# Stores in one row, loads on a second queue, zeros sent early and the choice of experts moved in an attention and mixture-of-experts kernel

## The chip, the core and the metric

The kernel runs on one core of a Trainium2 chip. The metric is the time of one execution in microseconds (us) on the device, taken in three runs; one further execution was recorded by the hardware profiler. The core has five engines with their own instruction streams: TensorE (PE, matmuls), VectorE (DVE), ScalarE (ACT), GpSimd (POOL) and SyncE (SP, which here only issues transfers). They meet through semaphores. Transfers are issued from SP, ACT or POOL and run on 16 DMA engines. PSUM has eight banks of 128 x 512 numbers.

## What is computed

The input `x` has 2 x 1024 tokens of width 256. From its layer norm `xn` two things are computed and both are added to `x`.

```python
qkv = xn @ qkv_w.T + qkv_b                       # 16 heads of 16
scores = einsum(q, k) / 4 + slope * (key - query), causal
x += softmax(scores) @ v @ out_w.T + out_b
# mixture of experts on the same xn
scores = sigmoid(xn @ gate_w)                    # 16 experts
selected = top_k(scores + expert_bias, 2)
w = scores[selected] / scores[selected].sum()
x += silu(xn @ shared_gate) * (xn @ shared_up) @ shared_down
x += sum over the two selected: w * (silu(xn @ g_e) * (xn @ u_e)) @ down_e
```

## The kernel before

The program is written out by hand for each engine; the order of each stream is the order of the code, and only semaphores tie the streams.

**Projections.** A list `JOBS` gives PE's work in turn, with one PSUM bank for each job: transposed weights and tokens, then 16 jobs of kind `qk` (one of q or k, 128 features, 512 tokens each), eight of `v`, four of the router's logits `g` and one of their transposes `r`. Each q/k result is split into three bf16 parts, so that bf16 matmuls keep f32 accuracy. ACT makes the first two parts (L594, L602), DVE the rest and the third (L750, L713). They stand in `parts`, a ring of `RING = 6` slots; SP stores slot `i % 6` to DRAM (`store_parts`, L379), and ACT may write part `i` only when store `i - 6` has landed.

**Head groups.** The 16 heads of two sequences are handled in `NG = 8` groups of four heads. For a group `load_group` brings the parts back in a layout in which one contraction over 108 or 111 rows holds all products of parts, the alibi terms and the negated row maximum (L337 and L339, 192, 128 and 64 KB and the alibi rows for each of q and k). It loads the first 512 positions and then the second, each with a semaphore of its own. Three buffers take the groups in turn. A group's maxima come first: PE computes scores (L1124, L1125), DVE reduces them (L888), DVE negates and splits the result (`negate`, L896 to L903), and SP writes it into three rows of the q buffer (`store_neg`, L408). Then PE computes the scores anew with the maximum subtracted (`exp_scores`, L1136), ACT takes the exponential (L665), and PE multiplies by the values (`weigh`, L1150). `ORDER` mixes, on PE and DVE, the exponential scores of group g with the maxima of group g + 1 and the first three (`EARLY`) of g + 2. Maxima have two slots in PSUM, so PE runs at most two ahead of DVE.

**Experts.** `route` on DVE picks two experts for each token and computes the two gates; `rank` on PE counts tokens by expert; `place` on DVE turns this into a row for each token and choice (`slot_i`) and an expert for each of the 48 tiles (`eid`). `sorted_tokens` is filled with zeros by 12 transfers (L402), POOL then scatters the tokens into it with 32 indirect transfers (L525), and after head groups 0 and 1 PE runs the 48 tiles. The shared expert (`shared_gate_up`, `shared_down`) is computed between the router and the attention, mixed with the maxima of group 0. The router's small tiles share SBUF with `ot_soon`, into which ACT evacuates attention outputs (`evacuate`, L669).

**SP's order** before the experts: constants, alibi rows, stores 0 to 5, load of group 0, stores 6 to 9, load of group 1, stores 10 to 15, zeros, negated rows of group 0, load of group 2, `w_gu` (the experts' first weights, 4 MB), negated rows of group 1, a wait for the scatters, `w_dn` (2 MB), four token tiles, load of group 3, negated rows of group 2.

## Time and profile before

| | us |
|---|---|
| three runs | 559.04, 561.94, 566.04 |
| median | 561.94 |
| profiled execution | 566.61 |
| its span, first to last instruction | 564.8 |
| PE busy | 476.7 (84%) |
| DVE busy | 327.7 (58%) |
| ACT busy | 247.5 (44%) |
| POOL busy | 141.3 (25%) |
| mean granted clock of TensorE | 0.906 |

The span is divided by the work into stages: projections to about 92 us, router to 110, shared expert and maxima of group 0 to 151, head groups 0 and 1 to 232, experts to 326, head groups 2 to 7 to about 533, and the output projection. A busy share is an average over these stages; which engine or queue sets the end of one is seen in the chain that ended last and in the waits of that stage. A releaser (`<-`) names what ended an engine's idle time. Lines such as L594 are lines of the kernel before.

### The profile page before, as it was taken

How to read it: one execution, taken by the hardware profiler on the slowest of the kernel's cores; microseconds unless marked ns; L12 is line 12 of the kernel's file. 1: busy time of each engine (PE TensorE's matmuls, PEld its weight loads, DVE VectorE, ACT ScalarE, POOL GpSimd, SP SyncE). 2: the span in 40 equal slices, each digit the busy share in tenths (PEclk: the TensorE clock that was granted, in tenths of full speed). 3: DMA queues.
4: the chain of work that ended last, by engine and by line, in shares of the span. 5: the costliest groups of instructions: out<-in, count | busy, mean ns of one | idle time of the engine just before them, and what ended most of it. 6: DMA issues, size and time to landing. Idle time of an engine off the chain costs nothing.

```text
span 564.8 us, 8563 instructions
## 1 busy us (share of the span) xinstructions
PE 476.7 (84%) x3049; PEld 271.4 (48%) x3049; DVE 327.7 (58%) x605; ACT 247.5 (44%) x567; POOL 141.3 (25%) x167
## 2 busy tenths in 40 slices
PE   4698069287599299799999999799999999699998
PEld 3587066154243143577777643344444353221476
DVE  4874076968867267354544477477776768422232
ACT  2663040000067167443444366466766767534400
POOL 2550000027740000000000058188875700000000
PEclk9799578689789789999999999799999999955899
DMA  9554433953334942144444233232332200010022
GB/s 274 92 167 127 130 107 123 387 198 110 107 130 124 310 156 75 54 150 141 139 141 140 94 103 109 76 110 58 111 99 84 88 12 1 4 13 0 2 76 75
DMA packets 64260, 63.53 MB, mean 112 GB/s; under 512 B 15295, under 2 KB 59907, under 8 KB 64219
## 3 DMA queue, kind: packets, MB, share of 16 engines
q1 hardware_dynamic: 60042, 54.18, 31.5%
q0 software_dynamic: 3072, 8.39, 4.6%
q8 instruction: 26, 0.43, 0.3%
q10 hardware_dynamic: 1104, 0.41, 0.3%
q14 instruction: 16, 0.12, 0.1%
HBM read 36.29 MB, written 26.15 MB: 111 GB/s over the span
## 4 chain that ended last, share of the span: by engine, by line
PE 65%; DVE 16%; DMA 7%; SPq 7%; ACT 3%; issue 2%; DVEq 0%; ACTq 0%
PE ps L1136 11%; PE ps L1150 11%; PE ps L1124 11%; PE ps L1074 9%; DVE mx L888 6%; PE ps L1170 5%; PE ps L1090 4%; SPq L337 4%; DMA qk<-nr 4%; SPq L408 2%; PE ps L974 2%; PE ps L1125 2%; PE ps L1139 2%; DMA qk_parts<-parts 2%; PE ps L1064 2%
## 5 line engine op out<-in xcount | busy, mean ns | idle before, releaser
L665 ACT ACTIVATE pt<-ps 128x512 f32<-128x512 f32 (+3 forms) x384 | 167.1, 492 | 132.3 <-PE ps L1139 103.8
L888 DVE TENSOR_REDUCE mx<-ps 128x1 f32<-128x384 f32 (+7 forms) x216 | 178.6, 864 | 71.4 <-PE ps L1125 69.4
L1136 PE MATMUL ps<-qk 111*128 111x512 bf16 (+3 forms) x384 | 117.0, 350 | 19.4 <-DMA qk<-nr 17.9
L1124 PE MATMUL ps<-qk 108*128 108x512 bf16 (+3 forms) x384 | 105.2, 342 | 9.5 <-DVE mx L888 8.9
L1150 PE MATMUL ps<-pt,vg 128*32 128x512 f32 (+3 forms) x768 | 86.8, 529 | 0.0
L1136 PEld LDWEIGHTS ps<-qk 111*128 111x128 bf16 x384 | 37.0, 101 | 72.5 <-ACT pt L665 23.8
L1124 PEld LDWEIGHTS ps<-qk 108*128 108x128 bf16 x384 | 32.7, 101 | 66.3 <-DVE mx L888 46.9
L541 POOL DMA_INDIRECT yg<-sorted_outputs,slot_i x32 | 32.3, 1011 | 104.7 <-DMA sorted_outputs<-y_out 96.5
L1125 PE MATMUL ps<-cbf 128*128 128x128 bf16 x256 | 56.0, 231 | 0.0
L1074 PE MATMUL ps<-w_gu,hx 128*128 x192 | 53.3, 401 | 2.0 <-ACT hx L633 1.3
L1139 PE MATMUL ps<-cbf 128*128 128x128 bf16 x256 | 54.2, 229 | 0.0
L876 DVE COPY y_out<-ps 128x256 f32<-128x256 f32 x48 | 20.4, 425 | 44.8 <-PE ps L1090 44.8
L525 POOL DMA_INDIRECT sorted_tokens<-xn,slot_i x32 | 31.0, 969 | 45.6 <-DMA sorted_tokens<-zeros 36.1
L514 POOL COPY vg<-v_sb 128x512 f32<-128x512 f32 x8 | 4.8, 609 | 143.0 <-PE ps L1150 94.2
L1074 PEld LDWEIGHTS ps<-w_gu,hx 128*128 128x128 f32 x192 | 32.5, 189 | 11.8 <-issue 8.0
L649 ACT ACTIVATE hx<-ps 128x384 f32<-128x384 f32 (+1 forms) x48 | 22.9, 477 | 26.1 <-PE ps L1064 24.5
L1125 PEld LDWEIGHTS ps<-cbf 128*128 128x128 bf16 x256 | 26.4, 103 | 15.9 <-issue 0.5
L1090 PE MATMUL ps<-w_dn,hx 128*128 x96 | 31.2, 406 | 0.9 <-ACT hx L649 0.9
L556 POOL TENSOR_SCALAR yg<-yg,gates 128x256 f32<-128x256 f32 x32 | 30.0, 938 | 3.4 <-DMA yg<-sorted_outputs,slot_i 2.2
L750 DVE SCALAR_TENSOR_TENSOR part_r<-ps,qkb,parts 128x512 f32<-128x512 f32 x16 | 11.9, 750 | 28.4 <-ACT parts L594 24.1
L974 PE MATMUL ps<-wh,xl 128*128 128x256 f32 x32 | 10.0, 313 | 21.1 <-DVE part_r L750 21.1
L1150 PEld LDWEIGHTS ps<-pt,vg 128*32 128x32 f32 x768 | 15.5, 111 | 22.7 <-ACT pt L665 16.1
(160 smaller groups left out, 577.4 us busy)
## 6 DMA issues: line engine op xcount, KB each, us to landing
qk_parts<-parts SPq DMA_DIRECT2D x16, 384.0 KB, 6.7
qk<-qk_parts SPq DMA_DIRECT2D x32, 192.0 KB
sorted_tokens<-zeros SPq DMA_DIRECT2D x12, 512.0 KB, 6.0
x_in<-sorted_tokens SPq DMA_DIRECT2D x48, 128.0 KB, 2.2
sorted_outputs<-y_out SPq DMA_DIRECT2D x48, 128.0 KB, 1.7
qk<-qk_parts SPq DMA_DIRECT2D x32, 128.0 KB
w_gu<-e_gu SPq DMA_DIRECT2D x1, 4096.0 KB, 19.4
x_sb<-x SPq DMA_DIRECT2D x4, 512.0 KB, 8.7
```

The source lines that it names most:

```text
L525: g_.indirect_dma_start(out=xsd, out_offset=bass.IndirectOffsetOnAxis(ap=slot_i[:, k, t:t + 1], axis=0), in_=xn[:, t, :], in_offset=None). ...
L541: g_.indirect_dma_start(out=yg[:, n % 4, :], out_offset=None, in_=ysd, in_offset=bass.IndirectOffsetOnAxis(ap=slot_i[:, k, t:t + 1], axis= ...
L556: g_.tensor_scalar(yg[:, n % 4, :], yg[:, n % 4, :], gates[:, k, t:t + 1], None, ALU.mult).then_inc(s_gw, 1)
L665: sc.activation(pt[:, s % 2, j, lo:CH], bank(n % 3)[:, lo:CH], ACT.Exp).then_inc(s_exp, 1)
L888: last = v.reduce_max(dst, src, axis=AX.X)
L1074: ins = te.matmul(bank(2 + w, 2 * F), hx[:, 1 - w, 1 + c, :], w_gu[:, bass.ds(e, 1), c, :].rearrange("p o f -> p (o f)"), start=c == 0, st ...
L1090: te.matmul(bank(4 + w, D), hx[:, w, 0, :], w_dn[:, bass.ds(e, 1), :].rearrange("p o f -> p (o f)"), start=True, stop=True).then_inc(s_dn, 1)
L1124: te.matmul(ps[:, at + c:at + e], q, k_buf[g % NBUF][0:K_MAX, j, c:e], start=True, stop=e < w)
L1125: ins = te.matmul(ps[:, at + w - P:at + w], idb, mask_q, start=False, stop=True)
L1136: ins = te.matmul(out[:, lo:CH], k_buf[g % NBUF][0:K_EXP, j, kb * P:(kb + 1) * P], q_buf[g % NBUF][0:K_EXP, j, qc * CH + lo:(qc + 1) * CH] ...
L1139: ins = te.matmul(out[:, lo:lo + P], idb, mask_k, start=False, stop=True)
L1150: ins = te.matmul(ps[32 * j:32 * j + 32, OUT_BANK * CH + lo:(OUT_BANK + 1) * CH], vg[:, par, kb, j, :], pt[:, s % 2, j, lo:CH], start=kb = ...
```

## The change

1. SP issues all 16 stores of q/k parts in one row. The loads of groups 0 and 1 are issued by POOL, once stores 0 to 3 and the alibi rows have landed, with semaphores of their own.
2. A load moves whole rows of 1024 positions: eight transfers for a group instead of 16, and PE waits once for all eight.
3. The zeros are issued before the alibi rows and the parts, once the constants have landed.
4. `route` and `place` on DVE come after the negation of group 0, `rank` on PE after the first eight exponential score blocks of group 0, in the PSUM bank of the attention output. `FIRST_ORDER` puts the maxima of group 1 that stood before that point behind it. DVE copies the ranks out of PSUM first.
5. The gates' sums over experts are made by POOL in ten small steps (`gate_sums`), and the division by their sum by four steps of DVE at the start of `experts`.

```diff
+RANKS_AT = ORDER.index(("out", 1))
+FIRST_ORDER = ([x for x in ORDER[:RANKS_AT] if x[0] != "max"] + [("rank", 0)] + [("max", 1, p) for p in range(EARLY)]
+               + [x for x in ORDER[:RANKS_AT] if x[0] == "max"] + ORDER[RANKS_AT:])
...
-        s_ld = [[sem(f"half{half}_loaded{n}") for n in range(NBUF)] for half in range(2)]
+        s_first = [sem(f"first_rows_loaded{n}") for n in range(NBUF - 1)]
+        s_ld = [sem(f"rows_loaded{n}") for n in range(NBUF)]
...
-        def load(queue, side, g, half):
+        def load(queue, side, g):
...
                 if side == 0:
-                    src = qkd[0, p0:p0 + 1, g:g + 1, :, :, cols].rearrange("n g d j s -> (g n) d j s")
-                    src = src.broadcast_to([n, HD, HG, CH])
+                    src = qkd[0, p0:p0 + 1, g:g + 1].rearrange("n g d j s -> (g n) d j s")
+                    src = src.broadcast_to([n, HD, HG, S])
...
+        def await_rows(queue, g):
+            if g < NBUF - 1:
+                queue.wait_ge(s_first[g], LOADS * DMA)
+            else:
+                queue.wait_ge(s_ld[g % NBUF], (g // NBUF + (g % NBUF == NBUF - 1)) * (LOADS * DMA))
...
             sp.dma_start(wsd[:, :], sd_w).then_inc(s_wo, DMA)
 
+            sp.wait_ge(s_zero, 2)
+            sp.wait_ge(s_c, DMA * N_CONST)
+            sp.wait_ge(s_wo, 4 * DMA)
+            sp.wait_ge(s_ws, 3 * DMA)
+            xz = xsd.rearrange("(p k) d -> p (k d)", p=P)
+            for n in range(NT // 4):
+                sp.dma_start(xz[:, n * 4 * D:(n + 1) * 4 * D], zeros[:, :, :].rearrange("p k d -> p (k d)")
+                             ).then_inc(s_clear, DMA)
...
-                for half in range(2):
-                    for side in range(2):
-                        load(sp, side, g, half)
+                for side in range(2):
+                    load(sp, side, g)
 
-            for i in range(RING):
+            for i in range(NQK):
                 store_parts(i)
             sp.wait_ge(s_auxst, 4 * DMA)
-            for i in range(4):
-                sp.wait_ge(s_parts[i], DMA)
-            load_group(0)
-            for i in range(RING, RING + 4):
-                store_parts(i)
-            load_group(1)
-            for i in range(RING + 4, NQK):
-                store_parts(i)
...
+            def gate_sums():
+                pool.wait_ge(s_picked, 1)
+                for k in range(K_TOP):
+                    summing(g_.tensor_tensor(weight[:, :, :], pick[:, k, :, :], prob[:, :, :], ALU.mult))
+                    for w in (E // 2, E // 4, E // 8):
+                        summing(g_.tensor_tensor(weight[:, :, 0:w], weight[:, :, 0:w], weight[:, :, w:2 * w], ALU.add))
+                    summing(g_.tensor_tensor(gates[:, k, :].unsqueeze(2), weight[:, :, 0:1], weight[:, :, 1:2], ALU.add))
...
+            pool.wait_ge(s_auxst, 4 * DMA)
+            for i in range(4):
+                pool.wait_ge(s_parts[i], DMA)
+            for g in range(NBUF - 1):
+                for side in range(2):
+                    load(pool, side, g)
             pool.wait_ge(s_free, JOBS.index(("g", 0, 0)))
             copy_v(0)
             copy_v(1)
 
+            gate_sums()
             pool.wait_ge(s_slot, 1)
...
             def evacuate(g, qc):
+                if g == 0 and qc == 0:
+                    act.wait_ge(s_slot, 2)
+                    act.wait_ge(s_gsum, GATE_STEPS)
...
                 dve.wait_ge(s_rank, 1)
-                ranks = bank(R0 % 8)
+                v.tensor_copy(ranks[:, :], bank(OUT_BANK, TT * E + E)).then_inc(s_ranks, 1)
+                dve.wait_ge(s_ranks, 1)
...
             def experts():
+                dve.wait_ge(s_gsum, GATE_STEPS)
+                v.scalar_tensor_tensor(gsum[:, 0, :], gates[:, 0, :], 1e-20, gates[:, 1, :], ALU.add, ALU.add
+                                       ).then_inc(s_gate, 1)
...
+            route()
+            place()
             for p in range(EARLY):
                 maxima(1, 1, p)
...
-                    for kind, a, b in [(*x, 0)[:3] for x in ORDER]:
+                    for kind, a, b in [(*x, 0)[:3] for x in (ORDER if g + par else FIRST_ORDER)]:
+                        if kind == "rank":
+                            rank()
+                            await_rows(pe, 1)
...
-                            if b in (0, FIRST_HALF):
-                                pe.wait_ge(s_ld[int(b > 0)][n % NBUF], (n // NBUF + 1) * (LOADS * DMA))
+                            if b == 0 and n > 1:
+                                await_rows(pe, n)
...
             shared_gate_up(0)
             shared_gate_up(1)
-            rank()
...
-                    pe.wait_ge(s_free, NJ)
-                    for half in range(2):
-                        pe.wait_ge(s_ld[half][0], LOADS * DMA)
+                    pe.wait_ge(s_free, NJ - 1)
+                    pe.wait_ge(s_prob, 1)
+                    await_rows(pe, 0)
```

**Order on SP**, the projections. `parts` are the stores, `qk<-qk_parts` the loads, `zeros` the clearing of the sorted tokens. Before:

```order
L371 DMA aux_rows<-aux 120x1024 [waits aux_ready] x4
L379 DMA qk_parts<-parts 128x3x512 [waits parts_ready] x6
L337 DMA qk<-qk_parts 48x4x512 [waits parts_stored2,parts_stored1,parts_stored3,parts_stored0,aux_stored]
...
L379 DMA qk_parts<-parts 128x3x512 [waits parts_ready] x4
L337 DMA qk<-qk_parts 48x4x512
...
L379 DMA qk_parts<-parts 128x3x512 [waits parts_ready] x6
L402 DMA sorted_tokens<-zeros 128x1024 [waits zeroed]
L402 DMA sorted_tokens<-zeros 128x1024 x11
L408 DMA qk<-nr 1x32x128 [waits neg_ready]
```

With the change, up to the wait of `w_dn`:

```order
L384 DMA wsd<-sd_w 128x256
L392 DMA sorted_tokens<-zeros 128x1024 [waits wo_loaded,small_weights_loaded,consts_loaded,zeroed]
L392 DMA sorted_tokens<-zeros 128x1024 x11
L397 DMA aux_rows<-aux 120x1024 [waits aux_ready] x4
L405 DMA qk_parts<-parts 128x3x512 [waits parts_ready] x16
L419 DMA qk<-nr 1x32x128 [waits neg_ready,aux_stored]
...
L445 DMA w_gu<-e_gu 128x32x256
L419 DMA qk<-nr 1x32x128 [waits neg_ready]
L419 DMA qk<-nr 1x32x128 x2
L448 DMA w_dn<-e_dn 128x16x256 [waits tokens_sorted]
```

The loads of groups 0 and 1 are gone from SP, the zeros stand ahead of the alibi rows and the 16 stores are in one row; `w_dn` waits for the scatters as it did before.

**Order on DVE**, from the logits to the first maxima of group 1. `rt<-prob` begins the choice, `slot_i` ends the placing of tokens. Before:

```order
L758 TENSOR_TENSOR v_sb<-ps,vb 128x2x4x64 [waits job_ready] x8
L741 COPY logits_t<-ps 16x512 [waits job_ready] x4
L784 TENSOR_SCALAR rt<-prob 128x256 [waits router_exp_ready,job_ready]
L785 RECIPROCAL prob<-rt 128x256 [waits router_step]
L786 TENSOR_TENSOR biased<-prob,eb 128x256 [waits router_step]
...
L822 CAST slot_i<-slot_f 128x32 [waits router_step]
L824 TENSOR_TENSOR etab<-cnt,row 128x768
L825 TENSOR_REDUCE eid_f<-etab 128x48 [waits router_step]
L826 TENSOR_SCALAR eid<-eid_f 128x48 [waits router_step]
L853 SCALAR_TENSOR_TENSOR th<-th,ps 128x512 [waits shared_tanh_ready]
L858 SCALAR_TENSOR_TENSOR hsh<-th,ps 128x512 [waits shared_step]
```

With the change (L885 and L890 are the shared hidden steps, L943 ends the negation of group 0, L928 are maxima):

```order
L796 TENSOR_TENSOR v_sb<-ps,vb 128x2x4x64 [waits job_ready] x8
L782 COPY logits_t<-ps 16x512 [waits job_ready] x4
L885 SCALAR_TENSOR_TENSOR th<-th,ps 128x512 [waits shared_tanh_ready]
L890 SCALAR_TENSOR_TENSOR hsh<-th,ps 128x512 [waits shared_step]
...
L943 TENSOR_TENSOR nr<-nrf,nr 32x128 [waits neg_step]
L822 TENSOR_SCALAR rt<-prob 128x256 [waits router_exp_ready]
L823 RECIPROCAL prob<-rt 128x256 [waits router_step]
...
L854 CAST slot_i<-slot_f 128x32 [waits router_step]
L856 TENSOR_TENSOR etab<-cnt,row 128x768
L857 TENSOR_REDUCE eid_f<-etab 128x48 [waits router_step]
L858 TENSOR_SCALAR eid<-eid_f 128x48 [waits router_step]
L928 TENSOR_REDUCE mx<-ps 128x4 [waits max_scores_ready]
```

The choice and the placing have moved from ahead of the shared expert to behind the negation of group 0.

**Order on PE**, the start of head group 0. L1136 and L1178 are exponential scores, L1124 and L1166 maxima of group 1, L1150 and L1194 `weigh`, L1025 the ranks. Before:

```order
L1136 MATMUL ps<-qk 128x512 [waits exp_done,vg_ready,neg_loaded0]
L1139 MATMUL ps<-cbf 128x128
L1124 MATMUL ps<-qk 128x384 [waits max_slot_freed]
L1125 MATMUL ps<-cbf 128x128
L1124 MATMUL ps<-qk 128x384 [waits max_slot_freed]
L1125 MATMUL ps<-cbf 128x128
L1136 MATMUL ps<-qk 128x512 [waits exp_done]
L1139 MATMUL ps<-cbf 128x128
...
L1136 MATMUL ps<-qk 128x384 [waits exp_done]
L1139 MATMUL ps<-cbf 128x128
L1150 MATMUL ps<-pt,vg 32x512 [waits out_evacuated,exp_done]
L1150 MATMUL ps<-pt,vg 32x512 x3
```

With the change:

```order
L1178 MATMUL ps<-qk 128x384 [waits exp_done]
L1181 MATMUL ps<-cbf 128x128
L1178 MATMUL ps<-qk 128x384 [waits exp_done]
...
L1025 MATMUL ps<-picked,cbf 128x16 [waits picked_ready,consts_loaded]
L1025 MATMUL ps<-picked,cbf 128x16 x15
L1027 MATMUL ps<-picked,cbf 128x256
...
L1166 MATMUL ps<-qk 128x128 [waits max_slot_freed,first_rows_loaded1]
L1167 MATMUL ps<-cbf 128x128
...
L1166 MATMUL ps<-qk 128x512 [waits max_slot_freed]
L1167 MATMUL ps<-cbf 128x128
L1194 MATMUL ps<-pt,vg 32x512 [waits ranks_evacuated,out_evacuated,exp_done]
L1194 MATMUL ps<-pt,vg 32x512 x3
```

Ten maxima of group 1, of which three stood ahead of the first exponential scores and seven between the eight blocks, now stand together between the ranks and the first `weigh`.

## Rows read from the trace of the kernel before

**Rows 1.** ACT timeline: start us, length us, engine, line, what, [idle before <- releaser]
```profile
40.45 0.69 ACT L594 ACTIVATE parts<-ps,qkb 128x512 bf16<-128x512 f32 x1 [3.42 <-DMA qk_parts<-parts]
...
46.99 0.67 ACT L594 ACTIVATE parts<-ps,qkb 128x512 bf16<-128x512 f32 x1
...
73.27 0.69 ACT L594 ACTIVATE parts<-ps,qkb 128x512 bf16<-128x512 f32 x1 [24.69 <-DMA qk_parts<-parts]
...
76.84 0.67 ACT L594 ACTIVATE parts<-ps,qkb 128x512 bf16<-128x512 f32 x1
...
99.35 0.60 ACT L628 ACTIVATE th<-ps 128x512 f32<-128x512 f32 x1 [2.19 <-PE ps L974]
```

**Rows 2.** SP queue timeline (issues of transfers), same columns, first 116 us
```profile
19.89 0.46 SPq L366 DMA_DIRECT2D wsd<-sd_w  x1
...
43.64 2.79 SPq L337 DMA_DIRECT2D qk<-qk_parts  x3
...
100.74 14.59 SPq L402 DMA_DIRECT2D sorted_tokens<-zeros  x12
```

**Rows 3.** Windows: stretch and length us, PE busy, PE clock, DMA share, GB/s
```profile
40.00:45.00 5.00, 5.00 (x24) 1.00 1.00 344
...
49.80:66.00 16.20, 3.97 (x34) 0.76 0.23 70
...
100.00:118.00 18.00, 7.59 (x58) 0.62 1.03 396
```

**Rows 4.** DMA issues: out<-in, queue, count, KB each, median us to landing
```profile
wsd<-sd_w SPq DMA_DIRECT2D x1, 128.0 KB, 3.4
...
qk<-nr SPq DMA_DIRECT2D x24, 8.0 KB, 1.9
...
sorted_tokens<-xn,slot_i POOLq DMA_INDIRECT x32, 2.4
```

**Rows 5.** DVE timeline, from the router to the first negated maxima
```profile
92.51 0.29 DVE L784 TENSOR_SCALAR rt<-prob 128x256 f32<-128x256 f32 x1 [1.82 <-ACT prob L586]
...
100.11 0.42 DVE L796 TENSOR_TENSOR picked<-pick 128x256 bf16<-128x256 f32 x1
...
107.72 0.18 DVE L822 CAST slot_i<-slot_f 128x32 int32<-128x32 f32 x1
...
109.89 0.68 DVE L853 SCALAR_TENSOR_TENSOR th<-th,ps 128x512 f32<-128x512 f32 x1
...
116.02 4.08 DVE L888 TENSOR_REDUCE mx<-ps 128x4 f32<-128x512 f32 x7 [0.16 <-PE ps L1125]
...
151.15 0.28 DVE L903 TENSOR_TENSOR nr<-nrf,nr 32x128 bf16<-32x128 f32 x1
```

**Rows 6.** PE timeline in the first two head groups
```profile
154.77 0.61 PE L1136 MATMUL ps<-qk 111*128 111x512 bf16 x1 [1.85 <-DMA qk<-nr]
...
161.39 1.06 PE L1150 MATMUL ps<-pt,vg 128*32 128x512 f32 x8
...
226.95 0.22 PE L1124 MATMUL ps<-qk 108*128 108x128 bf16 x1
```

**Rows 7.** SP queue timeline in the first two head groups
```profile
185.40 7.33 SPq L408 DMA_DIRECT2D qk<-nr  x3
...
192.77 0.58 SPq L437 DMA_DIRECT2D w_dn<-e_dn  x1
...
224.34 0.58 SPq L339 DMA_DIRECT2D qk<-aux_rows  x1
```

**Rows 8.** POOL timeline: first and last of the 32 scatters
```profile
122.77 1.23 POOL L525 DMA_INDIRECT sorted_tokens<-xn,slot_i  x1 [36.12 <-DMA sorted_tokens<-zeros]
...
162.26 0.96 POOL L525 DMA_INDIRECT sorted_tokens<-xn,slot_i  x1 [0.30 <-issue]
```

**Rows 9.** Chain that ended last: start us, length us, what
```profile
192.14 6.09 DMA qk<-nr
...
355.08 4.43 DMA qk<-nr
```

More of the change, by code:

```diff
@@ L1148, in weigh @@
                     pe.wait_ge(s_ev, g * 2 + qc + 1)
+                if g == 0 and s == 0:
+                    pe.wait_ge(s_ranks, 1)
                 for j in range(HG):
@@ L1204, in _ @@
                 if c == 0:
-                    pe.wait_ge(s_free, NJ)
-                    for half in range(2):
-                        pe.wait_ge(s_ld[half][0], LOADS * DMA)
+                    pe.wait_ge(s_free, NJ - 1)
+                    pe.wait_ge(s_prob, 1)
+                    await_rows(pe, 0)
                 for p in range(c * NP // 4, (c + 1) * NP // 4):
                     max_scores(0, 0, p)
-            for half in range(2):
-                pe.wait_ge(s_ld[half][1], LOADS * DMA)
-            for p in range(EARLY):
-                max_scores(1, 1, p)
             for g in range(0, NG, 2):
```

59 lines of the change are left out of this document (31 added, 28 removed).

## The prediction

> **What bounds the kernel now.** I read the page's chain that ended last first: PE carries most of it, so I looked in time order for its pieces that are not arithmetic. There are four. The longest is in the projections. ACT has all six slots of `parts` full and waits 24.69 us for a q/k part to be stored [rows 1]. SP, which issues the stores, is busy at that time with the 16 loads of head group 0 that it issues between store 5 and store 6; the first three are in [rows 2]. These loads move little: between 49.8 and 66 us the DMA engines are 23% busy at 70 GB/s, while six stores on their own run them full at 344 GB/s and the zeros at 396 [rows 3]. The reader should see a queue whose order costs time, not a lack of bandwidth. The second piece is the router on DVE, from 92.51 to 109.89 us [rows 5]; PE and ACT have nothing else for most of it. The third and fourth are waits of PE for the three small rows of negated maxima, which are queued behind large transfers: 6.09 and 4.43 us of transfer where 1.9 is the median [rows 4, 9].
>
> All times below are of the profiled execution, 566.6 us (span 564.8). It lies 0.8% above the median of the three runs, 561.94; the result is scaled to that at the end. N is the end of the first negation, 151.4 us before [rows 5].
>
> **1. Zeros ahead of the parts: a cost of 5 us.** The last constant before them is issued at 19.89 and lands 3.4 us after the issue ends [rows 2, 4], so the zeros start at about 23.8. They are 12 x 524 KB = 6.3 MB; at 396 GB/s [rows 3] that is 15.9 us, to 39.7. Behind them in the same queue go 0.98 MB of alibi rows (2.9 us at 344) and store 0 (1.1 us), then the landing, 1.9 us by the small stores of [rows 4]. Part 6 can start at about 46 instead of 40.45 [rows 1]. The scatter's old wait for the zeros, 36.12 us on POOL [rows 8], goes, but that POOL wait bounded nothing.
>
> **2. Stores in a row: a gain.** From part 6 on DVE sets the pace: from part 6 to part 11 it is 6.5 us (40.45 to 46.99 [rows 1]), and for the next four steps I take 1.5 each, a little over the mean of 1.3, so part 15 would start at 46 + 6.5 + 6 = 58.5 against 76.84: 18.3 us earlier. This is the lower bound of the cost. But POOL starts the 16 loads of groups 0 and 1 when parts 0 to 3 have landed, at about 49.5, and 3.5 MB then shares the engines with ten stores of 0.39 MB. All of that at 344 GB/s is 21.5 us, so if the stores came last, part 15 would start at 71, a gain of 5.8. The stores go out at 0.39 MB per 1.5 us, 260 GB/s, and need three quarters of the engines' time; I take 5 us of delay, nearer to the free end, since the loads of before left 77% of the engines idle. **Gain 13.3**, between 5.8 and 18.3. The loads themselves are hidden: POOL has 0.96 us per scatter and 1.27 from one to the next [rows 8]; 16 direct transfers at one to three times that are issued by 70 to 110, and group 0 is first read at about 90, group 1 at about 136.
>
> **3. The router leaves the front: a gain.** After the router's exponentials DVE now takes the shared hidden part at once. The second tanh ends at 99.95 [rows 1], the step that it feeds was reached at 111.2 (109.89 and two steps of the first tanh), and two additions and the first maxima follow at 116.02 [rows 5]. With PE no longer idle ahead of the shared down matmuls, that 116.02 becomes about 102.8. **Gain 13.2** (11 to 15). So N moves from 151.4 to 151.4 - 26.5 = 124.9.
>
> **4. The router in head group 0: a cost.** DVE needs 8.0 us up to `picked` and 9.4 from there to the end of the placing (109.89 - 100.53 [rows 5]); the gate products go to POOL, but the rank matmuls and a copy out of PSUM, once beside them, fill that time. PE meanwhile has only eight score blocks, after the 3.3 us of the negated rows' store (151.43 to 154.77 [rows 6]). Then it meets ten maxima in a row with two PSUM slots: the tenth needs eight reductions, 4.7 us by the seven in 4.08 of [rows 5], and its matmul. `weigh` of step 0 comes at N + 8.0 + 9.4 + 4.7 + 0.5 = N + 22.6, where it was N + 10.0 (161.39 [rows 6]). With 1 us for PE at the lower clock after its idle time: **cost 13.6** (11 to 17). Moving the router is thus nearly a wash.
>
> **5. The second group's negated rows: a gain.** Before, the negated rows of group 1 were issued from 185.40 on [rows 7], behind the 4.2 MB of `w_gu`, and landed at 198.2 (192.14 + 6.09 [rows 9]): 12.9 us after their negation instead of 3.3. Now that negation ends at N + 34.0 + 13.6 = N + 47.6. The load of group 2 starts at N + 2 and takes some 25 us (1.75 MB at 70 GB/s [rows 3]), `w_gu` behind it 12.2 at 344 GB/s and 2 to land, so it is through by about N + 41. **Gain 9.6** (5 to 9.6).
>
> **6. The load of group 3: a cost that the diff does not show.** The scatters now start after `slot_i`, at N + 8.0 + 7.2 = N + 15.2, and 32 of them take 40.5 us (122.77 to 163.2 [rows 8]), plus 2.4 to land [rows 4]: N + 58. SP waits for this before `w_dn`, and the load of group 3 stands behind. Before, the way from `w_dn` to the end of that load's issue was 192.77 to 224.92 [rows 7], 32.2 us, of which up to 4.8 were the rest of `w_gu`; with 27.4 to 32.2 and 1.9 of landing the rows are there at N + 87 to N + 92. PE asks for them at its first maxima of group 3, 75.5 us after N before (226.95 [rows 6]), now N + 75.5 + 13.6 - 9.6 = N + 79.5. Before, the first half sufficed there; now one semaphore counts all eight transfers. **Cost 9** (3 to 13).
>
> The load's size in time is the question. A row that bears on it is the 23% of [rows 3]: under four of 16 engines busy. The Trainium skill, "DMA: Bandwidth & Descriptors", section on why a DMA increments its semaphore by 16, says that a transfer runs on the largest number of engines up to 16 that divides the slowest dimension of both sides, here the leading 3 and 2 copies. The trace agrees (0.23 x 16 = 3.7). By that rule whole rows change nothing in the spread, and the load keeps its 25 us (1.75 MB at the 70 GB/s of [rows 3]).
>
> **7. Later groups.** The load of group 4 ended just ahead of the negated rows of group 3 and cost them 2.5 us (4.43 against 1.9 [rows 4, 9]); with half as many transfers I take it to be through. **Gain 2.5** (0 to 2.5; below zero by 2 if the whole load is late at the early maxima). Four small gate steps on DVE before the experts are hidden under the first token transposes and gate matmuls of PE, and ACT's new wait for POOL's ten small steps ends by N + 20: nothing. Were that cover gone they would cost some 1 us.
>
> **Sum:** -13.3 - 13.2 + 13.6 - 9.6 + 9 - 2.5 = -16.0, so 550.6; times 561.94 / 566.6 it is 546, and I forecast **547**.
>
> **Rivals.**
> - *The load is quick.* If the 23% came from 1 KB rows and not from the shape, a load with 8 KB rows takes 1.75 MB / 344 GB/s = 5 us, group 3 is in time and term 6 is gone: 566.6 - 25 = 541.6, **537** scaled. For it: the zeros' 4 KB rows moved at 396 against 344. Against it: that is 15%, not fivefold.
> - *Little is left.* Stores and loads share badly (5.8 instead of 13.3) and the load of group 3 is at its late end (12.5): -16 + 7.5 + 3.5 = -5, **557**. For it: both terms lean on estimates, and each stands at one place of the chain.
> - *POOL's loads starve the stores*: slower. A store needs all its engines; if an engine gives most of its turns to the 8 KB rows of a load, ten stores wait until the loads are through. At 25 us for a group two groups end at 49.5 + 50 = 99.5, part 15 starts at about 98, 21 us later than before instead of 13.3 earlier: 566.6 - 16 + 34.5 = 585, **580** scaled. It turns the sign once part 15 starts after 79.5, and passes 2% after 91. Against it: POOL's queue would have to put all these loads on the same few engines. The same page, section on queues, rings and completion order, says that an engine goes round its queues by packets; no row before shows two queues at full load.
> - *The change does not do what it says*: if part 6 to 15 still wait for something else on SP, gain 2 vanishes; SP's order leaves nothing there.
>
> **How the numbers follow.** My forecast has 0.52, with 540 to 555 of its own from the bounds of its terms; the quick load 0.14; little left 0.24; starved stores 0.08; the rest 0.02. The range 535 to 560 leaves out the starved case and the tails. About 2% (11.2 us, below 550.7) is what a measurement can tell from no change. Faster by that: 0.42 of the forecast, all of the quick load, 0.02 of little left, 0.58. Slower: 0.08. Within: 0.34.
>
> **What would show it.** Right: ACT's idle time before part 15 falls from 24.69 to under 15 us in all, and part 15 starts near 63; the first maxima near 90; a PE gap of some 7 us inside group 0 ended by DVE; no long wait for the negated rows of group 1; a PE wait of about 9 us for a transfer of `qk` ahead of the experts. Wrong: an ACT wait on stores while POOL's loads run that lasts beyond 79 us; maxima of group 0 or 1 that wait for rows; no wait ahead of the experts (quick load), or one over 13 us.

## The result, and the profile after

The changed kernel takes 588.88 us (median of four runs, 582.76 to 595.06) where the kernel before takes 561.32 (four runs, 559.04 to 566.04): ratio 1.0443, 95% interval 1.0325 to 1.0562. It is slower; I had forecast 547. Here and below, executions over 1.5% above the fastest of the same kernel stand in the medians and not in the ratios. The profiled execution took 582.76 us (span 580.8 against 564.8: 16.0 us more).

Part of what I expected is there: the first negation comes 17.9 us earlier, where I had 26.5. The loss is later. It is seen at once in the chain that ended last (page, part 4; before, PE had 65% and transfers 7%):

```profile
PE 40%; DMA 30%; DVE 9%; POOL 8%; SPq 7%; issue 4%; ACT 1%; DVEq 0%; ACTq 0%; POOLq 0%
DMA qk<-aux_rows 24%; PE ps L1116 9%; POOL sorted_tokens L560 5%; PE ps L1214 5%; PE ps L1194 5%; PE ps L1132 4%; PE ps L1178 4%; DMA qk_parts<-parts 4%; DVE mx L928 4%; PE ps L1016 3%; SPq L348 3%; PE ps L1166 3%; POOL aux L538 2%; PE ps L1106 2%; DMA eb<-ebias 1%
```

`qk<-aux_rows` is the last of a group's eight transfers, so it stands for the whole load. In the chain it has five pieces, one each for groups 3 to 7 (start, length, what):

```profile
200.95 26.77 DMA qk<-aux_rows
332.89 27.84 DMA qk<-aux_rows
370.07 27.84 DMA qk<-aux_rows
407.39 28.51 DMA qk<-aux_rows
445.23 26.34 DMA qk<-aux_rows
```

These lengths run from the issue of the last transfer. SP's queue, here for group 4, shows the first issue 4.3 us earlier, and the next load 37.2 us later:

```profile
328.59 1.94 SPq L348 DMA_DIRECT2D qk<-qk_parts  x3
...
332.89 0.53 SPq L350 DMA_DIRECT2D qk<-aux_rows  x1
...
365.79 1.93 SPq L348 DMA_DIRECT2D qk<-qk_parts  x3
```

PE's timeline has the waits at the first maxima of groups 3 to 7, 25.7 us in all:

```profile
227.76 0.29 PE L1166 MATMUL ps<-qk 108*128 108x128 bf16 x1 [8.73 <-DMA qk<-aux_rows]
...
360.78 0.29 PE L1166 MATMUL ps<-qk 108*128 108x128 bf16 x1 [5.36 <-DMA qk<-aux_rows]
...
397.97 0.29 PE L1166 MATMUL ps<-qk 108*128 108x128 bf16 x1 [4.12 <-DMA qk<-aux_rows]
```

The reader should see a closed loop. A load lasts 4.3 + 27.8 = 32.1 us. PE starts the next group's maxima only when all of it is there (360.7), needs 5.1 us from there until SP may overwrite the oldest buffer (365.79), and the next load begins. 32.1 + 5.1 = 37.2 us a group, and a faster PE could shorten only the 5.1. Before, from group 4 on, a group took 31.5: the negations of groups 5 to 7 ended at 422.1, 453.8 and 485.2 (that of group 4 at 390.7). DVE's timeline before has

```profile
421.79 0.28 DVE L903 TENSOR_TENSOR nr<-nrf,nr 32x128 bf16<-32x128 f32 x1
453.54 0.28 DVE L903 TENSOR_TENSOR nr<-nrf,nr 32x128 bf16<-32x128 f32 x1
484.88 0.28 DVE L903 TENSOR_TENSOR nr<-nrf,nr 32x128 bf16<-32x128 f32 x1
```

and now, for groups 3 to 7,

```profile
356.57 0.30 DVE L943 TENSOR_TENSOR nr<-nrf,nr 32x128 bf16<-32x128 f32 x1
...
394.58 0.33 DVE L943 TENSOR_TENSOR nr<-nrf,nr 32x128 bf16<-32x128 f32 x1
432.01 0.28 DVE L943 TENSOR_TENSOR nr<-nrf,nr 32x128 bf16<-32x128 f32 x1
469.74 0.28 DVE L943 TENSOR_TENSOR nr<-nrf,nr 32x128 bf16<-32x128 f32 x1
506.00 0.28 DVE L943 TENSOR_TENSOR nr<-nrf,nr 32x128 bf16<-32x128 f32 x1
```

The difference of the two spans by stage, from negation to negation (the first ends at N, 151.4 before and 133.5 after; differences of the unrounded times):

| stage | before | after | difference |
|---|---|---|---|
| start to N | 151.4 | 133.5 | -17.9 |
| to the negation of group 1 | 33.9 | 49.2 | +15.2 |
| to group 2 | 42.8 | 37.3 | -5.4 |
| to group 3 (experts between) | 125.7 | 136.8 | +11.1 |
| to group 7 | 131.3 | 149.4 | +18.1 |
| to the end | 79.7 | 74.6 | -5.1 |
| sum | 564.8 | 580.8 | +16.0 |

Of the 18.1 up to group 7 only 1.2 are in the first round, from group 3 to group 4: it took 36.9 us already before, where PE waited for negated rows (4.43 us of transfer [rows 9]), and 38.0 after. The other three rounds cost 16.9.

The gain at the end is TensorE's clock. PE is busy throughout 30 us of it in both kernels (501 to 531 before, 522 to 552 after); before, the granted clock was 0.50 in the first 15 of them (the level of 1.2 GHz) and 0.67 in the rest, after it was 0.55 and then 1.00 (2.4 GHz). Nothing of the change stands there, and a second trace of the changed kernel, `e15_change_again`, has 76.1 us for this stage.

In the projections the store waits of ACT, which answer to [rows 1], are

```profile
45.62 0.69 ACT L630 ACTIVATE parts<-ps,qkb 128x512 bf16<-128x512 f32 x1 [8.12 <-DMA qk_parts<-parts]
...
63.16 0.69 ACT L630 ACTIVATE parts<-ps,qkb 128x512 bf16<-128x512 f32 x1 [7.93 <-DMA qk_parts<-parts]
71.27 0.69 ACT L630 ACTIVATE parts<-ps,qkb 128x512 bf16<-128x512 f32 x1 [6.91 <-DMA qk_parts<-parts]
73.16 0.69 ACT L630 ACTIVATE parts<-ps,qkb 128x512 bf16<-128x512 f32 x1 [0.69 <-DMA qk_parts<-parts]
```

The wait before part 6 has grown from 3.42 us to 8.12, which is the price of the early zeros. The one wait of 24.69 us behind it is replaced by three that sum to 15.5, and part 15 starts at 73.16, 3.7 us earlier than before. What the DMA engines do meanwhile, by queue, from 49 to 70 us (packets, MB, share of the 16 engines), and the issues in that stretch:

```profile
q0 software_dynamic: 1971, 2.96, 50.3%
q1 hardware_dynamic: 2625, 2.58, 39.9%
...
qk_parts<-parts SPq DMA_DIRECT2D x7, 384.0 KB, 18.8
qk<-qk_parts POOLq DMA_DIRECT2D x4, 384.0 KB, 6.7
```

From POOL's queue the loads take half of all engines: the four transfers of 384 KB land in 6.7 us (median; the smaller ones in 8.3 to 19.3), while a store needs 18.8. On SP transfers with the same leading dimensions had left 77% of the engines idle [rows 3]. The packets of 4 and 8 KB in the trace hint at how. On POOL's queue five are under way at once for most of the first 1.6 us (its first two transfers have leading 3 and 2), and up to 15 in the next microseconds; of SP's load of group 5 there are two or three for most of the time from 374 to 397 us, never over five. That fits transfers that still use few engines each, but stand side by side on different ones; no run tests it alone.

### The profile page after: what moved, and what is told of

The parts are those of the page before. It is cut to its first block, busy times and chain, and to the rows that moved or that the text cites. A ratio compares the mean times of both kernels' runs of the same rounds, so it can differ in the third digit from the quotient of the medians.

```text
span 580.8 us, 8502 instructions
## 1 busy us (share of the span) xinstructions
PE 482.8 (83%) x3049; PEld 274.5 (47%) x3049; DVE 327.6 (56%) x602; ACT 246.9 (43%) x567; POOL 155.1 (27%) x193
## 4 chain that ended last, share of the span: by engine, by line
PE 40%; DMA 30%; DVE 9%; POOL 8%; SPq 7%; issue 4%; ACT 1%; DVEq 0%; ACTq 0%; POOLq 0%
DMA qk<-aux_rows 24%; PE ps L1116 9%; POOL sorted_tokens L560 5%; PE ps L1214 5%; PE ps L1194 5%; PE ps L1132 4%; PE ps L1178 4%; DMA qk_parts<-parts 4%; DVE mx L928 4%; PE ps L1016 3%; SPq L348 3%; PE ps L1166 3%; POOL aux L538 2%; PE ps L1106 2%; DMA eb<-ebias 1%
## 5 line engine op out<-in xcount | busy, mean ns | idle before, releaser
L928 DVE TENSOR_REDUCE mx<-ps 128x1 f32<-128x384 f32 (+7 forms) x216 | 178.8, 865 | 91.2 <-PE ps L1167 89.2
L1166 PE MATMUL ps<-qk 108*128 108x512 bf16 (+3 forms) x384 | 107.2, 347 | 43.2 <-DMA qk<-aux_rows 25.7
L1178 PE MATMUL ps<-qk 111*128 111x512 bf16 (+3 forms) x384 | 116.6, 350 | 11.7 <-DMA qk<-nr 10.2
L1194 PE MATMUL ps<-pt,vg 128*32 128x512 f32 (+3 forms) x768 | 88.5, 539 | 0.0
L1166 PEld LDWEIGHTS ps<-qk 108*128 108x128 bf16 x384 | 33.3, 103 | 103.1 <-DVE mx L928 56.6
L1178 PEld LDWEIGHTS ps<-qk 111*128 111x128 bf16 x384 | 37.7, 103 | 65.2 <-ACT pt L701 29.5
L1167 PE MATMUL ps<-cbf 128*128 128x128 bf16 x256 | 58.5, 240 | 0.0
L1181 PE MATMUL ps<-cbf 128*128 128x128 bf16 x256 | 55.8, 234 | 0.0
L560 POOL DMA_INDIRECT sorted_tokens<-xn,slot_i x32 | 31.2, 974 | 13.3 <-issue 13.3
L1167 PEld LDWEIGHTS ps<-cbf 128*128 128x128 bf16 x256 | 27.2, 106 | 15.7 <-issue 0.3
L1181 PEld LDWEIGHTS ps<-cbf 128*128 128x128 bf16 x256 | 27.0, 105 | 0.2
L1194 PEld LDWEIGHTS ps<-pt,vg 128*32 128x32 f32 x768 | 15.7, 112 | 22.7 <-ACT pt L701 13.7
L674 ACT ACTIVATE te_h<-ps 128x128 f32<-128x128 f32 x48 | 13.3, 277 | 28.8 <-PE ps L1116 28.8
```

The source lines that it names most:

```text
L560: g_.indirect_dma_start(out=xsd, out_offset=bass.IndirectOffsetOnAxis(ap=slot_i[:, k, t:t + 1], axis=0), in_=xn[:, t, :], in_offset=None). ...
L928: last = v.reduce_max(dst, src, axis=AX.X)
L1166: te.matmul(ps[:, at + c:at + e], q, k_buf[g % NBUF][0:K_MAX, j, c:e], start=True, stop=e < w)
L1167: ins = te.matmul(ps[:, at + w - P:at + w], idb, mask_q, start=False, stop=True)
L1178: ins = te.matmul(out[:, lo:CH], k_buf[g % NBUF][0:K_EXP, j, kb * P:(kb + 1) * P], q_buf[g % NBUF][0:K_EXP, j, qc * CH + lo:(qc + 1) * CH] ...
L1181: ins = te.matmul(out[:, lo:lo + P], idb, mask_k, start=False, stop=True)
```

## Experiments

Theories. **1**: PE waits once for all eight transfers, and a load of 32 us is longer than a group's arithmetic allows; rival: the whole rows themselves, or POOL's traffic, cost the time. **2**: a load is slow since each of its transfers runs on few engines; rival: it is bound by bytes or by row length. **3**: POOL's loads take the engines from the stores; rival: the stores hold each other up. **4**: moving the choice of experts is a wash.

The kernels ran on four chips, `e1` to `e4` on the first, `e5` to `e8` on the second, `e9` to `e12` on the third and the rest on the last, each beside the kernel before, which took 569.13, 587.58, 587.80 and 566.14 us there. So I compare inside a chip only.

**Waits and halves.** `e1_halves` is the changed kernel with the loads of groups 2 to 7 in two halves of 512 positions and a wait for each half; `e2_halves_onewait` has the same transfers, but PE waits for both halves at its first maxima.

```diff
-            for side in range(2):
-                load(sp, side, g)
+            for half in range(2):
+                for side in range(2):
+                    load(sp, side, g, (half,))
...
-    if b == 0 and n > 1:
-        await_rows(pe, n)
+    if b in (0, FIRST_HALF) and n > 1:         # e1 only; e2 keeps the line above
+        await_rows(pe, n, (int(b > 0),))
```

> The change, but the loads of groups 2 to 7 on SP again in two halves with a semaphore for each half, as in the kernel before; groups 0 and 1 stay whole rows on POOL. In the changed kernel PE waits for the whole load of groups 3 to 7 (8.7, 5.4, 4.1, 4.9, 2.6 us of idle time, 25.7 in sum) and the four rounds from one negation to the next take 37.4 us against 31.4 to 31.6. Theory 1 (the time is lost in these waits): they go, the rounds take 31.5 us again, 8.7 + 4 x 6 = 33 us less than the change: about 556 where the change has 589, no slower than the kernel before. Rival (the loss is made earlier, by the order of the projections, the router or the scatters, and the waits only take up slack): within 8 us of the change, 581 or more.

> As the kernel with half loads for groups 2 to 7, but PE waits for both halves at the first maxima, as the change does. It parts two causes of the late rows. Theory 1a (one wait instead of two is the cause): the load takes as long as whole rows, so PE still waits some 5 us in each of five groups, and the time is within 8 us of the change, 581 to 597. Theory 1b (whole rows make the transfers longer, 31 to 32 us from first issue to landing instead of some 25): the halves land in time, and the time is near that of the kernel with half loads and two waits, about 556 to 564.

Measured on one chip: 561.91 us (0.9878, 0.9784 to 0.9972) and 588.58 us (1.0384, 1.0298 to 1.0469). The number of waits alone makes 26.7 us. The first kernel is 1.2% faster than before, which is less than the 2% that I count as a change. In DVE's timeline of the first the negations of groups 5 to 7 end

```profile
422.19 0.28 DVE L951 TENSOR_TENSOR nr<-nrf,nr 32x128 bf16<-32x128 f32 x1
456.85 0.28 DVE L951 TENSOR_TENSOR nr<-nrf,nr 32x128 bf16<-32x128 f32 x1
488.26 0.28 DVE L951 TENSOR_TENSOR nr<-nrf,nr 32x128 bf16<-32x128 f32 x1
```

and in that of the second

```profile
439.92 0.28 DVE L951 TENSOR_TENSOR nr<-nrf,nr 32x128 bf16<-32x128 f32 x1
478.18 0.28 DVE L951 TENSOR_TENSOR nr<-nrf,nr 32x128 bf16<-32x128 f32 x1
515.51 0.28 DVE L951 TENSOR_TENSOR nr<-nrf,nr 32x128 bf16<-32x128 f32 x1
```

34.7 and 31.4 us apart against 38.3 and 37.3. PE's timeline has the cause. At the first maxima of group 3 it waits 1.25 us in the first kernel, and at those of groups 4 to 7 not at all; in the second the five waits sum to 35.9 us (the profile names no releaser for them). Here group 3 of the first, and groups 4 and 5 of the second:

```profile
220.81 0.23 PE L1174 MATMUL ps<-qk 108*128 108x128 bf16 x1 [1.25 <-DMA qk<-aux_rows]
```

```profile
366.91 0.27 PE L1174 MATMUL ps<-qk 108*128 108x128 bf16 x1 [7.17 <-issue]
405.09 0.26 PE L1174 MATMUL ps<-qk 108*128 108x128 bf16 x1 [4.14 <-issue]
```

The negation of group 7 ends 27.3 us apart in the two traces, but the stage behind it took 79.8 us in the first and 68.9 in the second, so the profiled executions (570.25 and 586.59 us) differ by less than the medians. That is the granted clock again: from 16 to 40 us into that stage it was 0.50 in the first and 1.00 in the second. Theory 1 holds, and the length of the rows is not the cause.

**That part alone.** `e5_before_whole` is the kernel before with whole rows, eight transfers and one wait for a group, all else as before.

```diff
-                if b in (0, FIRST_HALF):
-                    pe.wait_ge(s_ld[int(b > 0)][n % NBUF], (n // NBUF + 1) * (LOADS * DMA))
+                if b == 0:
+                    pe.wait_ge(s_ld[0][n % NBUF], (n // NBUF + 1) * (LOADS * DMA))
```

> The kernel before with one part of the change alone: a load moves whole rows of 1024 positions, eight transfers and one wait for a group; everything else as before. Theory 1 (the single wait for a load of some 31 us sets the rounds of groups 4 to 7): the negations of groups 4 to 7 lie 36 to 38 us apart instead of 31.5, the kernel is 20 to 30 us slower than before (1.035 to 1.053), and PE waits some 3 to 6 us a group for transfers of qk. Rival (the loss in the changed kernel comes from other parts of it, such as POOL's loads or the later zeros and scatters): within 1% of before, rounds of 31 to 33 us.

605.11 us against 587.58: 1.0322 (1.0237 to 1.0407). A little under the expected span of ratios, and the waits at the first maxima of groups 4 to 7 are 2.4 to 3.8 us where I had 3 to 6, but the mechanism is there without any other part of the change: its chain has loads of 26.1 to 27.4 us as pieces, and the negations of groups 4 to 7 lie 35.1 to 37.6 us apart.

**How many engines a transfer uses.** `e3_after_spread` is the changed kernel with six transfers of 16 partitions in the place of those of 48, 32 and 16; `e4_before_spread` does the same to the kernel before.

```diff
-            for t0, n in ((0, 3), (3, 2), (5, 1)):
-                ...
-                    src = src.broadcast_to([n, HD, HG, S])
-                ...
-                queue.dma_start(dst[HD * t0:HD * (t0 + n), :, :], src).then_inc(done, DMA)
+            for t, p in enumerate(order):
+                queue.dma_start(dst[HD * t:HD * (t + 1), :, :],
+                                qkd[side, p:p + 1, g:g + 1].rearrange("n g d j s -> (g n d) j s")).then_inc(done, DMA)
```

> The change, with each load made of six transfers of 16 partitions per side in place of three of 48, 32 and 16 (14 per group with the alibi rows, all whole rows, same bytes, same waits). Theory 2 (a load is slow because its transfers run on three and two of the 16 DMA engines, as the 23% busy share of the kernel before suggests): a load takes 6 to 9 us instead of 31, the waits of PE for rows are gone, and so is most of the waiting of ACT for stores behind the loads of groups 0 and 1; 33 to 43 us less than the change, 546 to 556. Rival (the load is bound by the issue on the queue or by the reading of DRAM): 14 transfers take no less than 8, the time stays within 8 us of the change or rises.

> The kernel before, with each half load made of six transfers of 16 partitions per side (28 per group, same bytes, same two waits, same order on SP). Theory 2 (engines used by a transfer): a group's load takes about 28 x 0.6 = 17 us of issue or less instead of 23 to 25; ACT's wait of 24.69 us for a store falls to 10 to 17, and the negated rows of group 1 and group 3 no longer queue behind a load: 10 to 30 us less, 531 to 551 where the kernel before has 561. Rival (issue or DRAM bound): more transfers, more issue: 561 or slower by up to 15.

548.41 us (0.9594, 0.9479 to 0.9709) and 538.19 us (0.9487, 0.939 to 0.9584), on the chip of the first pair. Twelve transfers with the same bytes make every wait of PE for loaded rows vanish, with rows of 8 KB and with rows of 1 KB. The packets of a load lie within 14 to 15 us in `e3_after_spread`, not the 6 to 9 that I expected, against 29.7 for group 5 in the changed kernel, and often 16 are under way at once. SP's issues are the price: in `e14_loads_after_stores_again`, further down, the 28 for one group take from 323.80 to 342.42 us, and that is still in time. With one wait in place the changed kernel gains some 7 to 8% on itself (ratio 0.9594 to before, against 1.0443 and, in `e15_change_again`, 1.0302). Theory 2 holds. The Trainium skill, "DMA: Bandwidth & Descriptors", section on why a DMA increments its semaphore by 16, says that the engine count is the largest number, up to 16, that divides the slowest dimension of both sides; the leading 3 and 2 of the old access patterns are replaced by 16, and these runs agree.

**Both together.** `e6_spread_halves` is `e3_after_spread` with halves and two waits.

> The changed kernel with every load in transfers of 16 partitions (six and the alibi rows for each side) and, in addition, groups 2 to 7 loaded in two halves with a wait each. Theory 2 (once a transfer uses all engines, the length of the rows and the number of waits do not matter): the same as with whole rows spread in this way, 0.955 to 0.97 of before. Rival (one wait costs in any case): 0.94 or less. A cost is possible too: SP issues twice as many transfers, at 0.6 us each, so 0.97 to 0.98 would say that the issue counts.

581.55 us against 587.58: 0.9878 (0.9836 to 0.992), worse than all that I expected. The rounds are right (31.4 to 31.9). The trace puts the excess elsewhere: between the first two negations there are 81.7 us, 49 in `e3_after_spread`. PE stands still there for 4.00, 14.28 and 9.77 us, the first two for nothing that the profile shows, until POOL's last scatter; a wait of 7.23 for DVE is in `e3_after_spread` too. Such a pause is in the traces of all kernels of this chip and the next, and in none of the others; it is taken up at the end. Of halves this run says only that they don't hurt the later rounds.

**Zeros late, router at the front**, each against `e1_halves`.

> The changed kernel with loads in halves, and with the zeros issued behind the 16 stores of parts instead of ahead of the alibi rows. By the prediction's term 1 the part in the seventh place starts 5 us earlier (about 40.5) and all behind it by as much, so about 5 us less than with the zeros early: 0.978 to 0.982 of before. Rival (the ten stores are bound by the engines' time while POOL's loads run, so that the last part starts when it did): 0.986 to 0.99, the last part still at about 73, because the zeros now meet the loads of groups 0 and 1.

> The changed kernel with loads in halves, and with the choice of experts, the ranks and the placing back ahead of the shared expert; the early maxima of group 1 are back in front of its exponential scores. Beside it stands the same kernel with the choice inside group 0 (0.988 of before). By the prediction's terms 3 and 4 (13.2 gained at the front, 13.6 lost in group 0) the two are equal within 3 us. By the traces of the two spread kernels (14.7 earlier at the first negation, 16.4 longer to the second) this one is 1 to 3 us faster. Rival (the move is worth something, since it hides DVE's chain behind PE's scores): this one 5 to 10 us slower, 0.995 to 1.005 of before.

`e8_halves_zeros_late` issues the zeros behind the 16 stores: 585.04 us (573.51 to 586.79) beside 587.58 of before, without an interval, so its time decides nothing. In its trace part 6 starts at 40.53, 5 us earlier as expected, but part 15 at 70.60, against 72.81 with early zeros on the same chip (`e7_halves_router_front`): of 5 us only 2.2 come through, the rest is given back to POOL's loads, nearer to the rival. `e7_halves_router_front`: 590.58 us, 0.9985 (0.9933 to 1.0037). The partner with the choice in group 0 had run on another chip, without the pause, so this pair decides nothing about the move. It was done again (below).

**Loads behind the stores.** `e9_spread_row_front_late`: the row of stores, POOL's loads, spread transfers in halves, late zeros, the choice at the front. `e10_loads_after_stores` differs from it in one wait of POOL:

```diff
-            for i in range(4):
-                pool.wait_ge(s_parts[i], DMA)
+            for i in range(RING):
+                pool.wait_ge(s_parts[i], DMA * len(range(i, NQK, RING)))
```

> All 16 stores in one row and the loads of groups 0 and 1 on POOL, as in the change, but with transfers of 16 partitions, halves for groups 2 to 7, the zeros behind the stores, and the choice of experts back at the front. Theory (the stores in one row are worth keeping once the rest is undone): part 15 starts at 63 to 66 us, 0.5 to 3 us a wait, and the kernel is 3 to 8 us faster than the kernel before with spread transfers alone. Rival (the ten stores and the 3.5 MB of loads share the same engines, and what the row gains the contention takes): part 15 at 70 or later, and the two kernels within 2 us.

> The kernel with the row of stores, the choice at the front, late zeros and spread transfers, with one edit: POOL starts the loads of groups 0 and 1 only when all 16 parts have been stored, not when parts 0 to 3 have. If the loads are what held the stores up (term 2's 3.7 us instead of 13.3), ACT's waits for stores between part 7 and part 15 fall under 1 us in all and part 15 starts at 58 to 60 us; the loads are still in time for group 0, and the kernel is 3 to 8 us faster than with the loads at parts 0 to 3. Rival (the stores hold each other up: 0.39 MB each 1.5 us with a landing of 6 us and six slots): part 15 stays at 63 to 67, with waits of 3 us and more.

> The kernel before with transfers of 16 partitions, a second time, beside the kernels that are built on it, on the same chip: 0.949 of before if the earlier ratio holds. Group 0's loads stand in the middle of the stores, so ACT still waits some 15 us for one store near 64 us.

On one chip (before: 587.80): 570.40 us (0.9708, 0.9659 to 0.9757), 556.88 us (546.74 to 559.70, without an interval), and 568.63 us for the spread kernel before (0.9695, 0.962 to 0.977). So the row of stores with the loads beside it is worth nothing (e9 against e12; I had expected 3 to 8 us), and one wait more gives 13.5 us by the medians. The same kernel has 0.9487 on the first chip and 0.9695 here, so a ratio moves by 0.02 from one chip to another. ACT's part 15, first with the loads at part 4, then behind all stores:

```profile
66.83 0.69 ACT L633 ACTIVATE parts<-ps,qkb 128x512 bf16<-128x512 f32 x1 [7.09 <-DMA qk_parts<-parts]
```

```profile
51.42 0.67 ACT L633 ACTIVATE parts<-ps,qkb 128x512 bf16<-128x512 f32 x1
...
52.90 0.67 ACT L633 ACTIVATE parts<-ps,qkb 128x512 bf16<-128x512 f32 x1
```

13.9 us earlier (I had expected 58 to 60), at DVE's pace of 1.48 us a part and with no wait for a store after part 6. Theory 3 holds; that the stores hold each other up is excluded.

**The choice of experts, once more.** `e11_spread_router_front` is `e3_after_spread` with the choice, ranks and placing at the front.

> The changed kernel with transfers of 16 partitions and the choice of experts, ranks and placing back ahead of the shared expert; zeros early, whole rows and the row of stores as in the change. The same kernel with the choice inside head group 0 was 0.959 of before. By terms 3 and 4 of the prediction (13.2 gained, 13.6 paid) 0.958; by the distance of the first two negations in the traces (14.7 gained, 16.4 paid) 0.955. Rival (the move is worth having): 0.97 or more. The second negation lies some 33 us behind the first, not 49.

571.74 us, 0.9719 (0.967 to 0.9769), which by itself is where I had put the rival. But it ran on a chip with the pause, where the ratio of the spread kernel before is 0.02 higher too, so it can't be held against the 0.959 of the other chip. For this, three more runs on one chip: `e14_loads_after_stores_again` (e10's kernel), `e13_router_in_group0` (the same, but for where `route`, `place`, `rank` and the early maxima of group 1 stand), and the changed kernel itself.

> The kernel with the row of stores, loads of groups 0 and 1 on POOL behind all stores, spread transfers in halves and late zeros, but with the choice of experts, ranks and placing inside head group 0, as in the change. The only difference to the kernel beside it is that place. Prediction's terms 3 and 4 (gain 13.2, cost 13.6): the two are equal within 2 us. Rival A (the front is better: 14.7 gained, 16.4 paid in the earlier traces): this one 1 to 4 us slower. Rival B (the move hides DVE's chain, and pays when nothing else is late): this one over 4 us faster. In the traces: first negation 13 to 15 us earlier, second negation 48 to 50 us behind it instead of 33.

> The best kernel so far a second time, beside the changed kernel on one chip: 0.93 to 0.95 of before. Its last q/k part starts at 52.9 us, with no wait for a store after the seventh part.

> The changed kernel as it is, on the same chip as the other two, so that the distances can be read on one chip: 1.03 to 1.055 of before, rounds of groups 4 to 7 of 37 to 38 us, last q/k part at about 73 us.

531.03 us (0.9364, 0.9276 to 0.9452), 528.76 us (0.9307, 0.9213 to 0.9401) and 584.33 us (1.0302, 1.0189 to 1.0414), before 566.14. The move makes 2.3 us to the worse. The two intervals overlap, so theory 4 (equal) and rival A (1 to 4 us slower) can't be told apart; rival B, over 4 us faster, is excluded. DVE's negations of groups 0 and 1 with the choice inside group 0, and at the front:

```profile
120.36 0.28 DVE L946 TENSOR_TENSOR nr<-nrf,nr 32x128 bf16<-32x128 f32 x1
170.33 0.28 DVE L946 TENSOR_TENSOR nr<-nrf,nr 32x128 bf16<-32x128 f32 x1
```

```profile
129.02 0.28 DVE L948 TENSOR_TENSOR nr<-nrf,nr 32x128 bf16<-32x128 f32 x1
163.06 0.28 DVE L948 TENSOR_TENSOR nr<-nrf,nr 32x128 bf16<-32x128 f32 x1
```

8.7 us are gained, where I expected 13 to 15, and 15.9 paid. That is 7.2 to the worse and not 2.3, but the profiled execution of the first lay 6.3 us above its median. The changed kernel came out as expected: rounds of 36.4 to 37.9 us, part 15 at 73.09. `e14_loads_after_stores_again` is the fastest kernel of the study: 6.9% under before, 55.6 us under the changed kernel on the same chip.

## Why the prediction was wrong

- **Step 7, later groups: this step failed.** I put a gain of 2.5 us and, as the worst, a loss of 2 if the whole load were late. It was a loss of 18.1 from group 3 to group 7. I had the pieces: 1.75 MB at 70 GB/s, 25 us for a load, and one semaphore for all eight transfers. I used them at group 3 (step 6) and not at the four groups behind it, where the load is issued only once a buffer is free. Two things were wrong. I never added up the loop; in a loop a late load is not paid once but each round. And the load took 32.1 us where I had 25: with 25 the loop closes at 30.1, still under the 31.4 of a round, and by this sum would have cost nothing. Why the load took longer than 25 is not shown. That the one wait makes the loss is shown by `e2_halves_onewait` against `e1_halves` (26.7 us), and `e5_before_whole` shows that it needs no other part of the change.
- **Step 2, stores in a row: mis-sized**, 3.7 us for 13.3, outside my own bound of 5.8. I reasoned that the loads leave 77% of the engines idle, which is a row of SP's queue. On POOL's queue they took 50.3% of all engines. The Trainium skill, "DMA: Bandwidth & Descriptors", section on why a DMA increments its semaphore by 16, names an exception to its rule: on trn2 some direct copies of the software queue run on 16 engines. This trace does not bear it out for these loads: five packets under way at once at their start fit 3 and 2 engines, not 16 for each. The bound of 5.8, by bytes at 344 GB/s, was the nearer one, but the engines moved 265 GB/s while they shared. The rival of starved stores was right in kind (a store landed after 18.8 us), but not in size: part 15 at 73, not 98. The free end was right: without loads part 15 starts at 52.6 with late zeros (`e14_loads_after_stores_again`), so by my estimate at 57.8 with early ones, where I had 58.5.
- **Step 1, zeros early: right**, 45.62 for 46. That more than half of it is absorbed later is in `e8_halves_zeros_late`, where only 2.2 of 5.1 us are left at part 15.
- **Step 3: right**, 14.1 us (the first maxima 17.8 earlier, at 98.20, less the 3.7) for 13.2.
- **Step 4: right.** The first `weigh` of group 0 is at 157.53, N + 24.0, for N + 22.6 and 1 more. By the negation of group 1 the cost is 15.2.
- **Step 5: 5.9 for 9.6.** PE resumed 7.0 us behind the negation of group 1, not 3.3; it waited 4.54 us for the small rows. I had `w_gu` through by N + 41, which is 174.5; SP's queue, with the load of group 2 ahead of `w_gu`, still moved 36 to 58 GB/s from 163 to 187 us. In `e3_after_spread` it was empty from 163 us to the negated rows.
- **Step 6: right in size, in part by luck**, a wait of 8.73 us for 9. Both of its ends came later than I had put them: the rows were there at 227.72, N + 94.2 for N + 87 to 92, and PE asked at 219.0, N + 85.5 for N + 79.5, since the steps before it had cost more.
- **The rivals.** The quick load is excluded: whole rows took 32.1 us, not 5. My 0.08 for slower held one mechanism alone, starved stores, priced at one stage; the mechanism that decided stood as half a sentence inside a step that I had put down as a gain. It should have been the slower rival: one round is the load plus the way to a free buffer, 25 + 5 at the least, against 31.4. That stood within 2 us of the point where it decides, round after round.

With the loop repaired (`e1_halves`, 0.9878) the change gains some 7 us. My sum with step 2 and step 5 at their measured sizes is -16 + 9.6 + 3.7 = -2.7, and the halves take step 6's 9 down to 1.25 us of wait, which makes -10.5; near the 7, whose interval is 2 to 12. So what was left besides the loop was of the right size.

## What to carry to other kernels

Merging transfers and waits costs time when somebody uses the first part early, as PE does here: with a ring of buffers ask for the loop, time of the whole load plus time from its arrival to the next free buffer, and hold it against a round's arithmetic. Give a transfer a leading dimension of 16 before anything else is tuned: here that alone was worth 5% on one chip and 3% on another. A transfer that is harmless on one queue may not be on another, as here; start bulk loads that nobody needs yet behind the stores that somebody waits for.

## What the runs showed of the hardware

- Loads with leading dimensions of 3 and 2 take few engines from SP's queue (0.23 busy, 70 GB/s [rows 3]) and half of all from POOL's (50.3% beside 39.9% of stores), where several are under way side by side. An issue costs POOL 0.6 to 0.7 us. On SP three issues of half rows took 2.51 us with nothing of the load under way and 8.73 right behind (`e2_halves_onewait`, from 332.91), three of whole rows 1.94 and 1.84 in the changed kernel. What holds the issue of half rows back is not shown.
- Rows of 8 KB did not shorten a load on few engines: 32.1 us for a group, where 25 was my estimate from rows of 1 KB.
- The stage behind the last negation has the same work in all kernels, but took 68.8 us (`e5_before_whole`) to 80.1 (`e14_loads_after_stores_again`) in the traces. PE idles for about a third of its first 15 us in both, and the granted clock falls to 0.50 some 8 us into it; in the first trace it was back at 1.00 at 16 us, in the second at 40. The kernel of the second took 74.4 in its other trace (`e10_loads_after_stores`), so this moves between executions of one kernel.
- On two chips PE, DVE and ACT did little or nothing for some 18 to 28 us while POOL issued its 32 scatters, in all eight kernels that were profiled there, and the kernel before was 18 to 26 us slower than elsewhere. In `e10_loads_after_stores` an activation of the shared expert on ACT and POOL's last scatter are

```profile
135.15 0.60 ACT L667 ACTIVATE th<-ps 128x512 f32<-128x512 f32 x1 [33.09 <-remote]
```

```profile
133.18 0.96 POOL L563 DMA_INDIRECT sorted_tokens<-xn,slot_i  x1 [0.30 <-issue]
```

and the windows of that kernel, then of the same kernel on a chip without the pause, are

```profile
120.00:130.00 10.00, 0.00 (x0) 0.00 (x0) 0.00 (x0) 0.00 (x0) 7.56 (x9) 0.50 0.30 105
```

```profile
120.00:130.00 10.00, 6.06 (x33) 2.73 (x32) 9.24 (x14) 0.00 (x0) 7.56 (x9) 0.75 0.28 98
```

The scatters themselves run alike (7.56 us of POOL, 9 of them). No instruction transfer is recorded from 105 to 141 us in the first, so late code is a possible cause. It was not tested, another kernel has one in the middle of its pause (`e11_spread_router_front` at 122 us), and why two chips show it stays open.
